# A grouped convolution by unshifted blocks of eight positions, with its outer part moved by one partition by DMA

## What is computed

```python
# layer 0
out = einsum('boi,bih->boh', agg_w, x) + agg_b[:, :, None]     # a 64x64 mixing matrix for each sample
# ffn: base = x @ W_base.T + b; 8 experts of rank 16 weighted by a gate
# layer 1
out = conv_general_dilated(x, weight, (1,), [(4, 4)], feature_group_count=4)   # 9 taps, 64 channels, 4 groups of 16
out = out + (c @ c_weight.T)[:, :, None] + bias[None, :, None]
# ffn: the same form, the two best of 8 experts
x = x + ffn(out)
```

## Time and profile before

| | us |
|---|---|
| three timed runs | 2237.74, 2239.08, 2240.82 (median 2239.08) |
| profiled execution, its own time | 2237.36 |
| span of its instructions | 2235.6 |
| one step of layer 0 / of layer 1, in the loop | 16.1 / 18.0 |
| PE busy | 2193.0 (98%) |
| DVE / POOL / ACT busy | 1394.9 / 858.6 / 401.7 |

### The profile page before, as it was taken

How to read it: one execution, slowest core, us unless ns; L and a number is a source line. 1 busy time by engine, 2 the same in 40 slices (tenths; PEclk the granted TensorE clock), 3 DMA queues, 4 the chain that set the end, 5 groups by cost and what they waited for, 6 DMA issues and landing times.

```text
span 2235.6 us, 40989 instructions
## 1 busy us (share of the span) xinstructions
PE 2193.0 (98%) x13196; PEld 2142.6 (96%) x13196; DVE 1394.9 (62%) x3667; ACT 401.7 (18%) x923; POOL 858.6 (38%) x1053
## 2 busy tenths in 40 slices
PE   4999999999999999999999999999999999999998
PEld 4999999999999999999999999999999999999998
DVE  6777777777777777776655555555555555555554
ACT  3221212121222222222211111111111111111110
POOL 5544444434343434344433333333333333333332
PEclk9999999999999999999999999999999999999999
DMA  5312121111112111213433333334433333333432
GB/s 168 117 60 79 61 73 66 70 70 69 70 69 70 69 70 64 75 60 111 105 93 89 88 88 88 88 88 99 98 94 90 88 88 88 88 88 96 97 95 62
DMA packets 134114, 189.48 MB, mean 85 GB/s; under 512 B 16080, under 2 KB 98384, under 8 KB 134096
## 3 DMA queue, kind: packets, MB, share of 16 engines
q1 hardware_dynamic: 133792, 188.69, 30.3%
q10 hardware_dynamic: 304, 0.56, 0.1%
HBM read 122.01 MB, written 67.18 MB: 85 GB/s over the span
## 4 chain that ended last, share of the span: by engine, by line
PE 96%; DVE 2%; DMA 1%; ACT 1%; issue 0%; POOL 0%; DVEq 0%; SPq 0%; ACTq 0%
PE psB L807 73%; PE psB L833 8%; PE psT L787 7%; PE psT L781 3%; PE psT L789 3%; PE psT L782 1%; PE psB L820 1%; POOL Wlo L324 0%; DVE small L666 0%; DMA outb<-in_condw 0%; DVE prod L526 0%; DMA attb<-att_scratch 0%; ACT Whi L443 0%; DMA Xraw<-in_x 0%; DVE Ylo L575 0%
## 5 line engine op out<-in xcount | busy, mean ns | idle before, releaser
L807 PE MATMUL psB<-Whi,Yhi 128*128 128x384 f32 (+2 forms) x3072 | 748.6, 352 | 3.6 <-issue 3.6
L333 POOL TENSOR_TENSOR Xlo<-Xraw,Xhi 128x256 fp32r<-128x256 f32 (+1 forms) x512 | 423.6, 859 | 785.0 <-ACT Xhi L417 785.0
L807 PE MATMUL psB<-Whi,Ylo 128*128 128x384 f32 (+2 forms) x3072 | 712.3, 340 | 0.0
L807 PE MATMUL psB<-Wlo,Yhi 128*128 128x384 f32 (+2 forms) x3072 | 708.6, 339 | 0.0
L807 PEld LDWEIGHTS psB<-Whi,Ylo 128*128 128x128 f32 x3072 | 558.3, 189 | 0.0
L807 PEld LDWEIGHTS psB<-Wlo,Yhi 128*128 128x128 f32 x3072 | 557.0, 189 | 0.0
L807 PEld LDWEIGHTS psB<-Whi,Yhi 128*128 128x128 f32 x3072 | 517.5, 190 | 19.5 <-issue 3.7
L566 DVE TENSOR_TENSOR Y<-psT,row 128x256 f32<-128x256 f32 x512 | 216.6, 423 | 338.3 <-PE psT L789 318.4
L362 POOL TENSOR_TENSOR res<-res,bias 128x256 f32<-128x256 f32 x256 | 181.5, 742 | 435.5 <-DMA res<-x_scratch 435.5
L431 ACT CAST Yhi<-Y 128x512 fp32r<-128x512 f32 x256 | 159.3, 622 | 897.3 <-DVE Y L568 897.3
L605 DVE TENSOR_TENSOR outb<-psB,res 128x384 f32<-128x384 f32 (+1 forms) x384 | 227.6, 678 | 72.2 <-PE psB L833 65.4
(11 more groups left out here) (85 smaller groups left out, 1397.7 us busy)
## 6 DMA issues: line engine op xcount, KB each, us to landing
Xraw<-in_x SPq DMA_DIRECT2D x64, 512.0 KB, 3.3
x_scratch<-outb SPq DMA_DIRECT2D x64, 512.0 KB, 2.6
Xraw<-x_scratch SPq DMA_DIRECT2D x512, 64.0 KB, 3.5
res<-x_scratch SPq DMA_DIRECT2D x64, 512.0 KB, 4.7
out<-outb SPq DMA_DIRECT2D x64, 512.0 KB, 3.0
row<-row_scratch SPq DMA_DIRECT2D x128, 64.0 KB, 3.1
stage<-in_l0w SPq DMA_DIRECT2D x8, 580.5 KB, 8.5
stage<-in_l1w SPq DMA_DIRECT2D x8, 580.0 KB, 6.2
```

What stands on the lines that cost most here:

```text
L333: last = pool.tensor_tensor(Xlo[:, piece], Xraw[:, par, piece], as_f32(Xhi[:, piece]), ALU.subtract)
L807: last = mm(psB[:, 3 * par + b, 0:cols], y, w[:, k, BANK0[b]:BANK0[b] + cols], start=(k == 0 and y is yh and w is Whi), stop=(k == KT - 1 ...
```

## The change

The blocks of X are no longer shifted: a tile is loaded with 128 columns for each piece, without padding. The weights `CT` now hold, for each group, [hi, lo] by [inner, outer] by 128 columns: the inner part gives what a block adds to its own 8 output positions, the outer part what it adds to its neighbours (positions 0 to 3 of the block behind it, 4 to 7 of the block before it). `mix(c)` has for each piece three matmuls of 256 columns. All of the sum lies in PSUM, so that the evacuation on DVE is one addition (inner part, plus constant) for each c.

The outer part is copied by ACT from PSUM into `side` (`copy_side`), moved by one partition from `side` into `shifted` by four DMAs of SP for each half (`shift`: rows 0 to 111 and 112 to 126, in both directions), and added to Y by DVE (`add_shifted`, 128x512). A half is here the pieces 0 to 3 or 4 to 7. `side` takes the place of `mixT` and `prod`, which layer 1 does not use. `shifted` is zeroed once by POOL. `base(0)` in layer 1 waits for both halves of Yhi and Ylo. POOL's zeroing of padding columns is gone.

```diff
@@ SP
+                if lay1 == 1:
+                    for h in range(2):
+                        shift(*after(j, par), h)
                 if lay0 is not None:
                     store(*before(j, par), lay0)
+            def shift(j, par, h):
+                m = 2 * j + par - STEPS
+                sp.wait_ge(side_out, NC * m + 2 * h + 2)
...
+                    sp.wait_ge(y_sum, 2 * m + h - 1)
+                for p0, p1 in SHIFT_ROWS:
+                    sp.dma_start(shifted[p0 + 1:p1 + 1, h, 0:REACH, :], side[p0:p1, h, 0:REACH, :])\
+                        .then_inc(side_in, 16)
+                    sp.dma_start(shifted[p0:p1, h, REACH:BR, :], side[p0 + 1:p1 + 1, h, REACH:BR, :])\
+                        .then_inc(side_in, 16)
@@ ACT
+            def copy_side(j, par, c):
+                act.wait_ge(y_chunk, NC * (m + STEPS) + c + 1)
...
+                nc.scalar.copy(to[:, b:b + 2], bank[:, :, 1]).then_inc(side_out, 1)
...
+                for c in range(NC):
+                    if last_of_0:
+                        split_w(c, 1)
+                    if lay1 == 1:
+                        copy_side(*after(j, par), c)
                 if lay1 is not None:
                     split_y(*after(j, par), lay1, range(0, 1))
+                if lay1 == 1 and lay0 is not None:
+                    high_ht(*before(j, par))
                 if lay2 is not None and not last_of_0:
                     high_x(j + 1, par, lay2)
@@ DVE, evacuate_y in layer 1
-                    nc.vector.tensor_tensor(y, parts[0], add, ALU.add).then_inc(y_part, 1)
-                    dve.wait_ge(y_part, NC * n + c + 1)
-                    nc.vector.tensor_tensor(y, parts[1], y, ALU.add).then_inc(y_chunk, 1)
+                        nc.vector.tensor_tensor(y, bank[:, :, 0], add, ALU.add).then_inc(y_chunk, 1)
+            def add_shifted(j, par, h):
+                m = 2 * j + par - STEPS
+                dve.wait_ge(side_in, SHIFTS * (2 * m + h + 1))
+                dve.wait_ge(y_chunk, NC * (m + STEPS) + 2 * h + 2)
+                y = y_half(Y[:, :], 1, h)
+                nc.vector.tensor_tensor(y, shifted[:, h, :, :], y, ALU.add).then_inc(y_sum, 1)
@@ PE
+                if layer == 1 and not (isinstance(j, int) and n == STEPS and c < 2):
+                    pe.wait_ge(side_out, NC * (n - STEPS) + c - 1)
...
+                        hi, lo = (CT[:, k % G, s, :, :].rearrange("p w n -> p (w n)") for s in range(2))
+                        mm(to, Xhi[:, xs], hi, start=True, stop=False)
+                        mm(to, Xhi[:, xs], lo, start=False, stop=False)
+                        last = mm(to, Xlo[:, xs], hi, start=False, stop=True)
...
+                if layer == 1 and k == 0:
+                    pe.wait_ge(yhi_half, 2 * n + 2)
+                    pe.wait_ge(ylo_half, 2 * n + 2)
```

More of the change, by code:

```diff
@@ L36 @@
 G, GC = 4, 16
-TAPS, PAD = 9, 4
+TAPS, REACH = 9, 4
 BR = 8
@@ L88, in build @@
         CT = sb("CT", [P, G, 2, 2, P], F32R)
+        shifted = sb("shifted", [P, 2, BR, HALF_B * GC])
         bias = sb("bias", [P, H])
-        Xraw = sb("Xraw", [P, 2, XW])
-        Xhi, Xlo = sb("Xhi", [P, XW], F32R), sb("Xlo", [P, XW], F32R)
+        Xraw = sb("Xraw", [P, 2, H])
+        Xhi, Xlo = sb("Xhi", [P, H], F32R), sb("Xlo", [P, H], F32R)
         Y = sb("Y", [P, H])
@@ L98, in build @@
         attb = sb("attb", [P, STEPS, MODES])
-        mixT = sb("mixT", [P, MODES, C])
-        prod = sb("prod", [P, MODES, C])
+        mixbuf = sb("mixbuf", [P, 2, MODES * C])
+        mixT, prod = (mixbuf[:, i, :].rearrange("p (k o) -> p k o", k=MODES) for i in range(2))
+        side = mixbuf[:, :, :].rearrange("p h (t n) -> p h t n", t=BR)
         agg = sb("agg", [P, C])
@@ L319, in _ @@
             pool.memset(stage[:, :, NW - 1:NW], 0.0).then_inc(consts, 1)
+            pool.memset(shifted[:, :, :, :], 0.0).then_inc(side_zero, 1)
             def split_lo(k, layer):
@@ L328, in low_x @@
                 n = 2 * j + par
-                w = (H if layer == 0 else XW) // PIECES
+                w = H // PIECES
                 pool.wait_ge(x_hi, n + 1)
@@ L428, in split_y @@
                 for h in halves:
-                    act.wait_ge(y_chunk, NC * n + (2 * h + 2 if layer == 0 else NC))
-                    nc.scalar.copy(Yhi[:, par, h * HB:(h + 1) * HB], Y[:, h * HB:(h + 1) * HB])\
-                        .then_inc(yhi_half, 1)
+                    if layer == 0:
+                        act.wait_ge(y_chunk, NC * n + 2 * h + 2)
+                    else:
+                        act.wait_ge(y_sum, 2 * (n - STEPS) + h + 1)
+                    nc.scalar.copy(y_half(Yhi[:, par, :], layer, h), y_half(Y[:, :], layer, h)).then_inc(yhi_half, 1)
+            def copy_side(j, par, c):
+                m = 2 * j + par - STEPS
+                act.wait_ge(y_chunk, NC * (m + STEPS) + c + 1)
+                if isinstance(m, int) and m == 0:
+                    act.wait_ge(agg_ready, STEPS)
+                else:
+                    act.wait_ge(side_in, SHIFTS * (2 * m + c // 2 - 1))
+                bank = psT[:, c % 2, :].rearrange("p (b s t o) -> p b s t o", b=2, s=2, t=BR)
+                to = side[:, c // 2, :, :].rearrange("p t (b o) -> p b t o", b=HALF_B)
+                b = 2 * (c % 2)
+                nc.scalar.copy(to[:, b:b + 2], bank[:, :, 1]).then_inc(side_out, 1)
             def split_w(k, layer):
@@ L734, in step @@
                     split_y(*after(j, par), lay1, range(0, 1))
+                if lay1 == 1:
+                    add_shifted(*after(j, par), 0)
                 if lay1 is not None:
@@ L741, in step @@
                     add_rest(*before(j, par))
-                if lay1 is not None:
+                if lay1 == 0:
                     split_y(*after(j, par), lay1, range(1, 2))
+                if lay1 == 1:
+                    add_shifted(*after(j, par), 1)
                 if lay2 == 0:
@@ L749, in step @@
                     emit(*before(j, par), lay0)
+                if lay1 == 1:
+                    split_y(*after(j, par), lay1, range(1, 2))
             run(dve, step)
```

81 lines of the change are left out of this document (37 added, 44 removed).

## The result

| | before | after |
|---|---|---|
| median (timed runs), us | 2238.46 (2237.74 to 2240.82, four) | 2336.02 (2334.24 to 2339.17, four) |
| profiled execution: span, us | 2235.6 | 2334.6 |
| one step of layer 1, in the loop, us | 17.98 | 19.36 |

The changed kernel takes 1.0435 times as long (95% interval 1.0417 to 1.0454). The forecast was 2218, with a range that ended at 2285. The time lies 51 us above that range, on the other side of no change.

What follows compares the result with a forecast made beforehand. Layer 1 was taken as bound by PE's own instruction stream; 63 steps x 0.38 = 24 us gained, 3 us added once: 2237.4 - 24 + 3 = 2216, and 1.7 for the median gives 2218, range 2201 to 2285.

Steps and rivals of the forecast that it cites:

- PE's part: `mix` in layer 1: six 256-column matmuls at 0.125 us each, 0.16 shorter; PE's own step falls 0.64 to 17.34.
- The rival of no faster matmuls: `mix` in layer 1: 256 columns cost 0.15, six cost what eight do; 2239 to 2245 us; chance 0.1.
- The way to the first issue: First half in layer 1: evacuation 1 at 4.86 us from step start, copy done 5.69, first shift issued 5.88.
- The value of x: Shifts of one half, first of four issues to last landing: 1.35 for issues plus 1.4 for landing, 2.75 us.
- The formula of the rival: Layer 1 step: shift time beyond 2.94 us enters twice, step 11.47 + 2x, slower than before; chance 0.3.
- The break-even x of 3.25: Layer 1 shifts: time from first issue to last landing at which the DMA-bound step is 17.98 us.
- Ylo behind `emit`: End of layer 1 step: second half's Ylo follows `emit`, reaching PE at 17.51, 0.17 later than PE's own 17.34.
- `up` isn't held: `up` in layer 1: HTlo ends at 12.03 us from step start, before `up` is due at 12.70.
- The start of layer 1: Step before layer 1: weight splits stand between the same links, one more Wlo on DVE; 3 us added once.
- Nothing else moves: Rest of the kernel: load count the same, `mix` of layer 0 and last step unchanged, zeroing runs while X loads.

Runs made afterwards that it cites:

- the kernels at 2.96 (17.3 us a step): The changed kernel with only the two 112-row pieces of each half, rows 112 to 126 left out of the sum: 2207.56 us, ratio 0.9859.
- Without the trip: The changed kernel without the eight shift DMAs of a step, the additions adding zeroed `shifted`: 2196.37 us, ratio 0.9807.

## Why the prediction was wrong, point by point

- **PE's part: right.** `base(1)` to `base(2)` is 2.31 us (1711.36 to 1713.67), foretold 2.34, before 2.51. A matmul of 256 columns costs 0.12, taken were 0.125. The rival of no faster matmuls falls.
- **The way to the first issue: right**, within 0.06 us at each link, as the timeline above shows. At the second trip the link from ACT's copy to SP's issue is 0.03 us (1720.63 to 1720.65) instead of 0.19.
- **The value of x: the step that failed.** It was 2.75 with bounds of 2.4 and 4.0, and is 4.2. Two terms were too small. Three distances between issues were taken as 3 x 0.45, since the new DMAs have constant addresses and SP issued its loads every 0.50; they are 2.2 in sum. A store is issued in 0.37 and a row load in 0.35, but a piece of 112 rows from SBUF to SBUF takes 0.55 to 0.6 and one of 15 rows 0.8 to 0.86. The landing of the last was taken as 1.4, built from the moments at which the store of layer 0 moved data, and is 2.0. Two of its three parts were good: 0.15 for the data and 0.4 behind it stand against 0.23 and 0.30. The part ahead of the data was taken as 0.85, as for the store, and is 1.47: the store's issue takes 0.35, that of 15 rows 0.82, and from its end to the first data another 0.65 pass. So in both terms it is mostly issue time that was too small, that of the 15-row pieces above all. The page's own rows had said 2.0 and 2.3 for small transfers; they were weighed down, as issued at the program's start, and they were the better guide. The Trainium skill's figure of about 2.0 us, which the prediction cited and then set aside, is given there for a DMA that GpSimd issues. It agrees with 2.0 (15 KB) and 2.3 (112 KB) on SP's queue here, and with 2.1 (15 KB) on GpSimd's.
- **The formula of the rival: right in form.** With x = 4.2, 11.47 + 2x gives 19.9; measured are 19.4. The second trip starts 0.2 earlier than the formula has it, the second addition takes 0.2 longer (0.89, beside POOL's Xlo), and `emit` and Ylo, which overlap by 0.1 to 0.2 with what is ahead of each, take 2.65 from the addition to PE instead of 3.08. The break-even x of 3.25 lies between the kernels at 2.96 (17.3 us a step) and 4.2, as it should. The rival had a chance of 0.3 and a range to 2311 that ended short, since its upper x was 3.8: it took the landing of 2.3 but not the slow issues. The stated range ended at 2285, an x of about 3.6, although the prediction's own upper bound was 4.0. With that bound the same formula gives 19.47 a step and 2336 us, which is what was measured; that it meets to the microsecond is luck, as a step 0.1 too long makes up for a start of layer 1 and a layer 0 that were too short.
- **Ylo behind `emit`: right that it is tight, 0.25 too slow.** Without the trip the step is 17.26, not 17.51: `emit` starts 0.1 earlier and Ylo starts before `emit` has ended.
- **`up` isn't held: wrong, without effect.** It waits 0.43 us for HTlo in the step above (0.30 in the median), hidden behind the second trip.
- **The start of layer 1: too small.** 9.2 us instead of 3: the shifts are issued behind the bias load and land behind it, and even without it the last one takes 3.6 us there.
- **Nothing else moves: nearly.** Up to the step before layer 1, 4 us more have gone by (2 to 6 in the kernels above), for a reason that isn't known.

## What to carry to other kernels

- Where a value makes a round trip through DMA inside a step, price it as the sum of the issue times ahead of the last one on that queue, plus one whole landing of the nearest small transfer on the page. If the landing is built up from parts, its first part is the transfer's own issue. A time per issue belongs to the form of the transfer, not to the queue: pieces of 16, 64, 96 or 112 rows cost 0.5 to 0.6 us here, pieces of 15 or 63 rows 0.74 to 0.86.
- Let the stated range reach as far as the bounds of its own terms. Here the bound of 4.0 for x was written down and the range stopped at 3.6.
- Look at what stands behind the wait on the waiting engine. Here the same late landing counted twice, since the next trip's first link was queued behind it; the order alone was worth 81 us.
- A change whose gain is real can be had once its cost is moved: with another order and a second queue the same idea gives 2206 us.

## What the runs showed of the hardware that was not expected

- From SP's queue 127 rows move on about one DMA engine (share 0.07, 24 GB/s, 13.6 us for two pieces); from GpSimd's queue 127 rows land after 2.2 us.
- The issue of a transfer on SP takes 0.51 to 0.60 us in the loop with 16, 64, 96 or 112 rows, 0.74 to 0.86 with 15 or 63. Of two with 127 rows the first takes 0.59 to 0.64 and the second mostly 1.1 to 1.3.
- A transfer of 15 rows from SP's queue moves its first data 1.47 us after its issue began (0.65 after the issue ended), and lands 0.30 us behind its last data.
- Eight more small transfers in each step beside the loads and stores cost 1.2 us in the whole kernel, as long as nobody waits for them.
